# Two causal attentions: scores of all banks first, transposes ahead of the values, copies split between ScalarE and VectorE

## The reference

```python
def _L0_attn_ref(x, wq, wk, wv, wo):          # 32 query heads of 16, 8 key/value heads
    q = bitlinear(x, wq).reshape(B, S, 8, 4, 16)
    k = bitlinear(x, wk).reshape(B, S, 8, 16)
    v = bitlinear(x, wv).reshape(B, S, 8, 16)
    scores = jnp.einsum('bskgd,btkd->bkgst', q, k) * sm_scale
    scores = jnp.where(causal, scores, -inf)
    probs = softmax(scores)
    out = jnp.einsum('bkgst,btkd->bskgd', probs, v).reshape(B, S, 512)
    return bitlinear(out, wo)

def _L1_xattn_ref(q, latent_kv, Wq, Wkv_expand, Wout):     # 16 heads of 32
    qp, (k, v) = q @ Wq.T, split(latent_kv @ Wkv_expand.T)
    scores = einsum('bhqd,bhkd->bhqk', qh, kh) * inv_sqrt_d    # causal
    out = einsum('bhqk,bhkd->bhqd', softmax(scores), vh)
    return out @ Wout.T

x = x + _L0_xattn_ref(_layernorm(x), ctx_512, ...)
x = x + _L0_attn_ref(_layernorm(x), ...)          # "attention 0"
x = x + _L0_ffn_ref(_layernorm(x), ...)           # 32 experts, top 8
x = x + _L1_xattn_ref(_layernorm(x), ctx_512, ...)  # "attention 1", keys are 64 rows
x = x + _L1_attn_ref(_layernorm(x), ...)
x = x + _L1_ffn_ref(_layernorm(x), ...)
```

## Time and profile before

| | |
|---|---|
| median of 3 runs | 376.07 us (375.77 to 376.51) |
| the profiled execution's own time | 375.67 us |
| its span, first to last instruction | 373.9 us |
| TensorE busy | 363.7 us, 97% |
| VectorE, ScalarE, GpSimd busy | 149.0, 92.0, 37.3 us |
| chain that ended last, by engine | PE 86%, DMA 6%, DVE 4%, SPq 2% |
| HBM traffic | 79.4 MB, 212 GB/s over the span |
| attention 0, scores to the end of the projection | about 140 to 158 us |
| attention 1, the same | about 284 to 298 us |

### The profile page before, as it was taken

One profiled execution on the slowest core, in us unless ns is written; L12 is line 12 of the kernel. 1 busy time (PEld: TensorE's weight loads), 2 busy tenths in 40 slices (PEclk: granted clock), 3 DMA queues, 4 the chain that ended last, 5 costly groups with the idle time before them and its releaser, 6 DMA issues.

```text
span 373.9 us, 5085 instructions
## 1 busy us (share of the span) xinstructions
PE 363.7 (97%) x2052; PEld 220.7 (59%) x2054; DVE 149.0 (40%) x333; ACT 92.0 (25%) x181; POOL 37.3 (10%) x74
## 2 busy tenths in 40 slices
PE   8998999999999999999999999999998999999997
PEld 6887577777776584565444444444336555554455
DVE  2129556676441146245122222222237245663131
ACT  1011433556441015012121221221103005230010
POOL 1006000000000010011000000000008420010310
PEclk9999999999999999999999999999999999999999
DMA  7999999800005100060898898899949940000000
GB/s 270 423 422 463 403 425 423 362 6 0 2 0 205 49 2 0 2 259 23 311 400 325 335 357 321 333 359 380 432 149 426 424 170 2 0 2 0 0 0 28
DMA packets 7798, 79.40 MB, mean 212 GB/s; under 512 B 992, under 2 KB 1760, under 8 KB 2912
## 3 DMA queue, kind: packets, MB, share of 16 engines
q1 hardware_dynamic: 7776, 79.09, 53.1%
HBM read 78.82 MB, written 0.26 MB: 212 GB/s over the span
## 4 chain that ended last, share of the span: by engine, by line
PE 86%; DMA 6%; DVE 4%; SPq 2%; issue 1%; ACT 1%; DVEq 0%; ACTq 0%
PE ps L1386 10%; PE ps L1532 9%; PE ps L1123 7%; PE ps L1146 7%; DMA ra<-in_wq 6%; PE ps L1413 4%; PE ps L1411 4%; PE ps L1215 4%; PE ps L1463 4%; PE ps L1135 4%; PE ps L1418 3%; PE ps L1373 3%; PE ps L1346 3%; PE ps L1328 2%; PE ps L1266 2%; PE ps L1024 2%
## 5 line engine op out<-in xcount | busy, mean ns | idle before, releaser
L1386 PE MATMUL ps<-rd,ra 128*64 128x384 f32 x224 | 39.2, 492 | 0.0
L1146 PEld LDWEIGHTS ps<-rd,ra 128*128 128x128 f32 x256 | 29.9, 192 | 4.4 <-issue 4.1
L1146 PE MATMUL ps<-rd,ra 128*128 128x128 f32 x256 | 31.3, 275 | 0.0
L1123 PE MATMUL ps<-rd 128*128 128x512 f32 x64 | 30.2, 594 | 0.0
L1386 PEld LDWEIGHTS ps<-rd,ra 128*64 128x64 f32 x224 | 14.8, 136 | 25.6 <-issue 25.6
L1532 PE MATMUL ps<-rd,xnT 128*128 128x512 f32 x64 | 28.0, 593 | 0.0
L464 ACT ACTIVATE ra<-ps,sv 128x1024 f32<-128x1024 f32 x16 | 17.9, 1116 | 35.0 <-DVE sv L706 35.0
L1024 PE MATMUL ps<-ones 128*128 128x256 bf16 x173 | 25.0, 292 | 1.0 <-POOL ones L382 1.0
L894 DVE COPY xnT<-ps 128x512 f32<-128x512 f32 x14 | 9.7, 692 | 38.8 <-PE ps L1413 38.8
L706 DVE TENSOR_REDUCE sv<-ps 128x1 f32<-128x1024 f32 x16 | 19.6, 1222 | 12.5 <-PE ps L1123 12.5
L1024 PEld LDWEIGHTS ps<-ones 128*128 128x128 bf16 x173 | 17.5, 104 | 7.3 <-issue 3.4
(11 more groups left out here) (256 smaller groups left out, 524.1 us busy)
## 6 DMA issues: line engine op xcount, KB each, us to landing
rd<-in_ring SPq DMA_DIRECT2D x16, 2304.0 KB, 9.0
rd<-in_f1gu SPq DMA_DIRECT2D x8, 1024.0 KB, 12.8
rb<-in_wb SPq DMA_DIRECT2D x1, 5120.0 KB, 35.9
ra<-in_e SPq DMA_DIRECT2D x2, 2560.0 KB, 16.9
rb<-in_b SPq DMA_DIRECT2D x1, 5120.0 KB, 20.7
ra<-in_wr SPq DMA_DIRECT2D x4, 1152.0 KB, 16.5
ra<-in_wq SPq DMA_DIRECT2D x3, 1024.0 KB, 16.3
ra<-in_f1s SPq DMA_DIRECT2D x1, 2048.0 KB, 27.3
```

The source lines that it names most:

```text
L1123: ins = pe.matmul(ps[:, 2 * (u % 2) + half, :], rows, kvT[:, u % 2, half * 512:half * 512 + 512], start=True, stop=True)
L1146: ins = pe.matmul(ps[:, 6, 0:P], probT_x[u % 2][:, j, :], kvr[:, u % 2, j, :], start=(j == 0), stop=(j == J - 1))
L1386: ins = pe.matmul(ps[CAP * e:CAP * e + CAP, 2 + p % 2, 0:2 * I0].rearrange("p (g n) -> p g n", g=2), moe_xq[q % 2][:, c, CAP * e4:CAP * e4 ...
```

## The change

All of it lies in the three `attention(a)` functions.

- TensorE, a = 0: the scores of all four banks, then the transposes of banks 0, 1 and 2, values 0, transposes 3, values 1, 2, 3. For a = 1: both banks' scores, both banks' transposes, both banks' values.
- The transposed banks go to PSUM banks 5, 6, 4, 2 instead of 5 and 6 in turn, so no transposes wait for an earlier copy.
- The filler products: for a = 0, 2 ahead of values 0 and of values 3 and 3 ahead of the output transposes (7, were 25); for a = 1, 7 ahead of each bank's transposes, 2 ahead of values 0, 3 ahead of each half of the output transposes (22, were 21).
- ScalarE copies the even banks (L527 before), VectorE the odd ones (new). ScalarE's order for a = 1 is exponential 0, copy 0, exponential 1.
- The output transposes are two pairs, to PSUM banks 1 and 5, each with its semaphore step. ScalarE copies the first pair, VectorE the second, 256 columns each. For a = 1 the first pair waits only for bank 0's division.
- The projection waits for ScalarE's half before its first product and for VectorE's half before its third.

The diff, cut to its core (renamed semaphores, and lines that only move into a function, are left out):

```diff
+        att_T_bank = (5, 6, 4, 2)
...
 ScalarE, attention(a)
-                for i in range(n + 2):
-                    if i < n:
-                        act.wait_ge(asub[a], i + 1)
-                        p = att_prob[a][:, i].rearrange("p h t -> p (h t)")
-                        act.activation(p, p, ACT.Exp, scale=exp_scale).then_inc(aexp[a], 1)
-                    if i >= 2:
-                        act.wait_ge(at2_ps[a], i - 1)
-                        act.activation(att_probT[a][:, i - 2]..., ps[:, 5 + i % 2, :],
-                                       ACT.Copy).then_inc(at2_sb[a], 1)
+                exp_bank(0)
+                if a == 0:
+                    exp_bank(1)
+                    exp_bank(2)
+                    probT_even_copy(0)
+                    exp_bank(3)
+                    probT_even_copy(2)
+                else:
+                    probT_even_copy(0)
+                    exp_bank(1)
+                act.wait_ge(aoT_ps[a], 1)
+                act.activation(att_oT[a][:, 0:2, :]..., ps[:, 1, 0:256], ACT.Copy,
+                               scale=sc_vo if a == 0 else 1.0).then_inc(at2_sb[a], 1)
...
 VectorE, attention(a), behind the maxima and differences of all banks
+                probT_odd_copy(1)
+                divide(0)
                 if a == 0:
-                    dve.tensor_scalar(oT, ps[:, 1, :], sc_vo, None, ALU.mult).then_inc(aoT_sb[a], 1)
+                    probT_odd_copy(3)
+                for m in range(1, n):
+                    divide(m)
+                dve.wait_ge(aoT_ps[a], 2)
+                oT = att_oT[a][:, 2:4, :].rearrange("p c t -> p (c t)")
+                if a == 0:
+                    dve.tensor_scalar(oT, ps[:, 5, 0:256], sc_vo, None, ALU.mult).then_inc(aoT_sb[a], 1)
                 else:
-                    dve.tensor_copy(oT, ps[:, 1, :]).then_inc(aoT_sb[a], 1)
+                    dve.tensor_copy(oT, ps[:, 5, 0:256]).then_inc(aoT_sb[a], 1)
...
 TensorE, attention(a)
+                def bank_transposes(m):
+                    if a == 1:
+                        keep_clock(7, 1)
+                    pe.wait_ge(aexp[a], m + 1)
+                    for j in range(4):
+                        ins = pe.transpose(ps[:, att_T_bank[m], j * P:(j + 1) * P], ...)
+                    ins.then_inc(at2_ps[a], 1)
+
+                def bank_values(m):
+                    if m == 0:
+                        pe.wait_ge(av_sb[a], 1)
+                    if m in (0, 3):
+                        keep_clock(2, 1)
+                    if m % 2 == 0:
+                        pe.wait_ge(at2_sb[a], m // 2 + 1)
+                    else:
+                        pe.wait_ge(akp_sb[a], m // 2 + 2)
+                    if m >= 2:
+                        pe.wait_ge(ao_sb[a], m - 1)
...
+                def output_transposes(half, banks):
+                    pe.wait_ge(ao_sb[a], banks)
+                    src = att_o[a].rearrange("p (c q) -> p c q", c=C)
+                    for c in range(2):
+                        ins = pe.transpose(ps[:, (1, 5)[half], c * P:(c + 1) * P], src[:, 2 * half + c, :], ident)
+                    ins.then_inc(aoT_ps[a], 1)
...
-                keep_clock(5, 3)
-                pe.wait_ge(ao_sb[a], n)
...
+                keep_clock(3, 3)
+                output_transposes(0, n if a == 0 else 1)
+                if a == 1:
+                    keep_clock(3, 3)
+                output_transposes(1, n)
+                residual(2, ln, True)
+                pe.wait_ge(at2_sb[a], 3 if a == 0 else 2)
                 for c in range(C):
-                    ins = pe.transpose(ps[:, 1, c * P:(c + 1) * P], src[:, c, :], ident)
-                ins.then_inc(aoT_ps[a], 1)
-                residual(2, ln, True)
-                pe.wait_ge(aoT_sb[a], 1)
-                for c in range(C):
+                    if c == 2:
+                        pe.wait_ge(aoT_sb[a], 1)
                     ins = pe.matmul(ps[:, 2, :], att_oT[a][:, c, :], e_wo[:, c, :], start=False, stop=(c == C - 1))
```

More of the change, by code:

```diff
@@ L770, in make_k @@
                                                     m32.unsqueeze(2).broadcast_to([P, 4, P]), ALU.mult)
-                    ins.then_inc(ak_sb[a], 1)
+                    ins.then_inc(akp_sb[a], 1)
                 def make_v():
@@ L819, in attention @@
-                dve.wait_ge(aoT_ps[a], 1)
-                oT = att_oT[a].rearrange("p c t -> p (c t)")
-                if a == 0:
-                    dve.tensor_scalar(oT, ps[:, 1, :], sc_vo, None, ALU.mult).then_inc(aoT_sb[a], 1)
+                for i in range(n):
+                    dve.wait_ge(as_ps[a], i + 1)
+                    s = ps[:, (3, 4, 2)[i % 3], :].rearrange("p (h t) -> p h t", h=8)
+                    mx = att_mx[i % 2]
+                    link(dve.tensor_reduce(mx, s, AX.X, ALU.max))
+                    dve.tensor_tensor(att_prob[a][:, i], s, mx.unsqueeze(2).broadcast_to([P, 8, S]),
+                                      ALU.subtract).then_inc(asub[a], 1)
@@ L1319, in attention, with bank_scores @@
[L1319 to L1327 removed]
+                def bank_scores(i):
+                    if i >= 3:
+                        pe.wait_ge(asub[a], i - 2)
+                    if i == 2:
+                        pe.wait_ge(av_sb[a], 1)
+                    bank = (3, 4, 2)[i % 3]
+                    pe.matmul(ps[:, bank, :], identb[:, :], maskb[:, :, :].rearrange("p h t -> p (h t)"),
+                              start=True, stop=False)
+                    chunks = [i] if a == 0 else [2 * i, 2 * i + 1]
+                    pe.wait_ge(aq_sb[a], chunks[-1] // 2 + (2 if a == 0 else 1))
+                    pe.wait_ge(akp_sb[a], 1)
+                    for m, c in enumerate(chunks):
+                        w = 512 // len(chunks)
+                        heads = range(0, 8) if a == 0 else range(4 * c, 4 * c + 4)
+                        for b in range(B):
+                            ins = pe.matmul(ps[S * b:S * b + S, bank, w * m:w * m + w].rearrange("p (h t) -> p h t", t=S),
+                                            att_qT[a][:, c, S * b:S * b + S],
+                                            att_kbd[a][:, heads[0]:heads[-1] + 1, S * b:S * b + S],
+                                            start=False, stop=(m == len(chunks) - 1))
+                    ins.then_inc(as_ps[a], 1)
@@ new lines, in bank_transposes @@
+                def bank_transposes(m):
[3 more added lines that the diff above has]
+                    for j in range(4):
+                        ins = pe.transpose(ps[:, att_T_bank[m], j * P:(j + 1) * P],
+                                           att_prob[a][:, m, 2 * j:2 * j + 2, :].rearrange("p h t -> p (h t)"), ident)
+                    ins.then_inc(at2_ps[a], 1)
+                def bank_values(m):
+                    if m == 0:
+                        pe.wait_ge(av_sb[a], 1)
+                    if m in (0, 3):
[6 more added lines that the diff above has]
+                        pe.wait_ge(ao_sb[a], m - 1)
+                    w = 2 * (hd + 1)
+                    for j in range(4):
+                        for b in range(B):
+                            ins = pe.matmul(ps[S * b:S * b + S, 7 if m % 2 == 0 else 0, j * w:j * w + w],
+                                            att_probT[a][:, m, j, S * b:S * b + S],
+                                            att_v[a][:, b, j if a == 0 else 4 * m + j].rearrange("p two e -> p (two e)"),
+                                            start=True, stop=True)
+                    ins.then_inc(ao_ps[a], 1)
@@ new lines, in output_transposes @@
+                def output_transposes(half, banks):
[4 more added lines that the diff above has]
+                    ins.then_inc(aoT_ps[a], 1)
+                if a == 0:
+                    bank_scores(0)
+                    bank_scores(1)
+                    bank_scores(2)
+                    bank_scores(3)
+                    bank_transposes(0)
+                    bank_transposes(1)
+                    bank_transposes(2)
+                    bank_values(0)
+                    bank_transposes(3)
+                    bank_values(1)
+                    bank_values(2)
+                    bank_values(3)
+                else:
+                    bank_scores(0)
+                    bank_scores(1)
+                    bank_transposes(0)
+                    bank_transposes(1)
+                    bank_values(0)
+                    bank_values(1)
```

89 lines of the change are left out of this document (22 added, 67 removed).

## The result

| | before | changed |
|---|---|---|
| median | 375.92 us (375.64 to 376.51, 4 runs) | 373.06 us (371.99 to 373.32, 4 runs) |
| ratio to before, 95% interval | | 0.9916 (0.9893 to 0.9940) |
| the same, second series | 376.11 us (28 runs) | 372.94 us (6 runs), 0.9921 (0.9905 to 0.9937) |
| profiled execution, its span | 375.67, 373.9 us | 371.99, 370.2 us |

The changed kernel is faster by 0.8%, 2.9 to 3.2 us. I had forecast 2.3 us, 373.8 us: the direction and the places were right, the size was too small.

A forecast was written before the change was run, and what follows sets the result against it. TensorE's path was taken to bound the kernel, at full clock. Gains of 1.87 us (attention 0), 0.25 (its output halves) and 0.2 (attention 1) sum to 2.3 us: 376.07 to 373.8 us, range 373.2 to 374.4, wider 372.9 to 375.2.

The forecast's parts named there:

- What bounds it: a saving in the middle moves all that follows: Whole program: the chain runs through TensorE, later loads are not in it, so time saved mid-program moves everything after it.
- Attention 0, scores and transposes: Attention 0: scores 3 directly after scores 2 gain 0.47 us; transposes 3 start at 147.96 instead of 149.45.
- Values 3 wait for VectorE's queue: Attention 0: copy 3, then division 1 (done 149.9) on VectorE replace fillers as the wait; values 3 at 149.96, before 151.83.
- Output halves, attention 0: 0.25 us: Attention 0's end: projection starts 1.25 us after the output transposes instead of 1.50, gaining 0.25 us.
- Attention 1: 0.15 to 0.25 us forecast: Attention 1: transposes 1 come 0.65 us late, fewer fillers ahead of values and the halves outweigh it; 0.15 to 0.25 us gained.
- 292.2 + 0.53 + 0.2 + 0.53 = 293.5: Attention 1, after values 1: three fillers, first output pair, three fillers, bringing TensorE to the second pair at 293.5.
- if fillers cost no idle beyond themselves, 0.5 us: Attention 1: the upper case, fillers at 0.11 us each without added idle, gaining 0.5 us.
- The sum and the range: Whole kernel: 2.3 us gained, bounds 1.9 to 2.75 us; 373.8 us, own range 373.2 to 374.4, chance 0.72.
- Rival 1: Attention 1 loses its 0.65 us from late transposes 1, halves give 0.25 back; 1.7 us gained, 374.4 us; chance 0.10.
- Rival 2: Both attentions: fillers only filled waits; 0.47 us from scores 3 and 0.25 from halves remain, 0.7 us gained, 375.4; chance 0.08.
- Rival 3: Whole kernel: saving lost at a later meeting point such as a load, no measurable effect, 375.8 to 376.3 us; chance 0.05.
- Rival 4: Attention 0, 7 fillers instead of 25: TensorE's clock falls, work takes 1.75 times as long, 1.7 us slower, 377.8; chance 0.05.

The follow-up runs named there:

- the last experiment: Changed kernel with values 3 in PSUM bank 3, no fillers ahead of them, and attention 1's exponential 1 before both copies on ScalarE: 371.19 us, ratio 0.9865.
- the kept trace: Trace of the changed kernel without any filler between scores and projection in both attentions: attention 0 13.25 us, attention 1 19.37 us, ratio 0.9941.

## Why the prediction was right and where it failed

- *What bounds it: a saving in the middle moves all that follows.* Right. The expert layer took 120.06 us and the tail 75.3 us in all traces, to 0.1 us.
- *Attention 0, scores and transposes.* Right. On the old clock (0.76 us added) transposes 3 came at 147.94 (I had 147.96), values 1 at 148.53 (148.35: TensorE is idle for 0.17 us between transposes and values, which I had left out without fillers), values 3 at 149.91 (149.96), output transposes at 151.21 (151.25). That values 3 still came on time is partly luck: values 1 and 2 stand behind each other in 1.01 us of loads (147.77), 1.05 us to the next filler, where I had twice 0.59, and this second error nearly makes up for the first.
- *Values 3 wait for VectorE's queue.* Right within 0.1 us. In the changed kernel division 1 ended at 149.01, and what held values 3 until 149.15 were the two fillers and the 0.21 us of idle behind them. Without fillers values 3 waited for the division, and attention 0 was only 0.08 us shorter; in a bank of their own they did not, and it was 0.45 us shorter.
- *Output halves, attention 0: 0.25 us.* The number is right, 0.25 by taking them away; the way to it was not. From the output transposes to the projection's first product it is 1.36 us (150.45 to 151.81), where I had 1.25, so 0.14 us are gained there. The other 0.11 lie in the projection: from its first product to the statistics it is 3.63 us instead of 3.74 (154.62 to 158.36 before), which I had not counted. ScalarE's half, 0.47 us with its scale, held the first weight load by 0.31 us but not the product, which waits for the residual anyway.
- *Attention 0 in all: 2.12 us forecast, 2.16 measured,* with the small errors above cancelling.
- *Attention 1: 0.15 to 0.25 us forecast, 0.76 measured. This is the step that failed.* Up to the fillers behind values 1 all came as I had it: transposes 1 1.95 us after transposes 0 (forecast 1.98), values 0 2.75 us after them (2.80), the first of the fillers 4.01 us (4.03). What failed is the term behind them, "292.2 + 0.53 + 0.2 + 0.53 = 293.5": three fillers ahead of each pair of output transposes, each group at 3 x 0.11 + 0.21 us. The 0.21 us came from a single stretch of the earlier trace rows in which values follow fillers. It belongs to the step into the values, not to the fillers: 0.17 us stand there without any filler too (147.77; 288.91 in the kernel without fillers). Ahead of transposes it is missing. The first group with its pair took 0.45 us (289.26 to 289.71, I had 0.73), and the second group was through by the time that division 1 ended, at 290.04; the second pair started at 290.10. So the bound was the division, the second pair came 4.85 us after transposes 0 instead of 5.32, and with it the projection. That nothing there hangs on the fillers is shown by the kernel without them: 19.37 us again. These 0.47 us are most of what was missing; another 0.10 us lie in the projection, as in attention 0 (3.64 us, 291.23 to 294.87, instead of 3.74). I had named the case "if fillers cost no idle beyond themselves, 0.5 us", and taken the dearer end.
- *The sum and the range.* 2.3 us forecast, 2.92 by the stretches. Nearly all of the difference is attention 1. The upper bound of the gain, 2.75 us, was too low as well, since its 0.5 us for attention 1 still had no room for 0.76; of the signs that I had named, that one (0.1 to 0.5 us in attention 1) was missed. The first profiled execution of the changed kernel had early loads on top (0.76 us).
- *Rival 1, attention 1 loses its 0.65 us.* The delay happened, 0.62 us, and turning ScalarE's order gives it back; but the fillers outweigh it, which are not fewer (22 for 21) but stand ahead of longer waits. At their old places attention 1 is 0.22 us slower than before, which is the rival, in a kernel that is not the changed one.
- *Rival 2, the fillers only filled waits.* Wrong for attention 0 as it was; with the trimming alone 0.89 of the 2.16 us come.
- *Rival 3, the saving is lost later.* It was not: the expert layer and the tail took the same time to 0.1 us.
- *Rival 4, the clock falls.* It did not fall in the changed kernel, with 29 fillers in the two attentions: 0.999 or more in all 10 executions. Without any it was full in the trace, and two of six executions had 0.995. The rule of the Trainium skill (TensorE: Matmul & The Clock Gate, "What's actually happening") that activity lifts the throttle is not contradicted; the waits of up to 1.53 us in that trace did not bring it back. The price that I had put on a fall, 1.75 times, was too low. It is the mean of a row that spans both levels: 21 loads of the 27 in the earlier trace rows, from 1.17 us on, take 4.42 us, 0.21 us each, and the last three come 0.11 us apart, so the step is nearly twofold.

## What to carry to other kernels

Filler work in front of a wait is free only as long as the wait is longer than it: compare the fillers' end with the end of what is awaited, in the trace, at every place, and reorder only together with trimming them: in attention 0 the order with the halves gave 0.2 us, the trimming 0.9, and all together 2.2. When pricing such a group, take the durations from a place with the same neighbours on both sides, ask which idle time would be there without the group, and let the next real wait bound the sum. On an engine that takes its work in order, put what the longest chain waits for first: one exchanged pair on ScalarE was worth 0.6 us.

## What the runs showed of the hardware that I had not expected

- Fillers cost 0.108 us each and nothing beyond, ahead of fp32 transposes (five in 0.45 us from load to load) and between transposes and 64-row products (0.74 us, of which 0.20 are there without them). Between two groups of 64-row products five took 0.65 us from load to load, 0.11 more than their own time; against groups with nothing between it is more still, by an estimate from rows about 0.76 us: in attention 0 before, values 2 and 3 start 1.25 us apart (150.58 to 151.83), and the three groups without fillers in the last experiment 0.49 us apart (48 loads in 1.48 us).
- TensorE was busy for 16.84 of 20 us, with waits up to 1.53 us, at a granted clock of 1.00 in the kept trace; two other executions of that kernel had a mean of 0.995.
- ScalarE copies a 128 x 512 fp32 bank from PSUM in 0.58 us, VectorE in 0.69 us, and ScalarE's next operation can start 0.50 us after the copy's start.
- The first weight loads scatter: the chain's load took 22.65 us in one execution of the changed kernel and 23.63 us in another and ended 1.9 us later there, more than half of what the whole change moves, while everything behind the loads repeats to 0.1 us.
